# Two mixture stages of a fused network kernel: the first tile's projections move between the gate groups, the softmax and the choice of experts split into two parts, and the last sums change engine

## The reference

```python
x = x + attn_a0(layernorm(x))      # window attention
x = x + mixture(layernorm(x))      # the block of this case
x = x + attn_b0(layernorm(x))      # causal attention
x = x + mixture(layernorm(x))      # the block of this case, once more
x = x + attn_a1(layernorm(x))
x = x + stack(layernorm(x))        # six layers of local attention and feed-forward
x = x + attn_b1(layernorm(x))      # linear attention
x = x + stack(layernorm(x))

def mixture(x):                    # 8 experts, 2 of them for each row
    scores = softmax(x @ gate_w.T)
    weights, idx = top_k(scores, 2)
    xs = x[:, None, :] * weights[:, :, None]
    for e in range(8):
        h = silu(xs @ w1[e].T + b1[e])
        x2 = h @ w2[e].T + b2[e]
        x3 = xs @ w3[e].T + b3[e]
        y = y + sum(x2 * x3 * (idx == e))
    return y + silu(x @ sw1.T) * (x @ sw2.T) @ sw3.T
```

## Time and profile before

| | us |
|---|---|
| median of 3 runs | 4148.89 |
| the three runs | 4132.82, 4240.24, 4148.89 |
| the profiled execution's own time | 4147.29 |
| its span, first to last instruction | 4145.5 |
| busy: PE, VectorE, ScalarE, POOL | 3791.3, 2998.6, 2593.4, 2693.0 |

### The profile page before, as it was taken

The page is one execution under the profiler, slowest core; times in us unless marked ns, Lnnn a source line. Parts: engine busy times, 40 slices in busy tenths (PEclk is TensorE's granted clock), DMA queues, the critical chain, the costliest instruction groups (busy, mean ns, idle before and its releaser), DMA issues. The chain is left out here.

```text
span 4145.5 us, 159706 instructions
## 1 busy us (share of the span) xinstructions
PE 3791.3 (91%) x67305; PEld 2643.7 (64%) x67305; DVE 2998.6 (72%) x6173; ACT 2593.4 (63%) x4984; POOL 2693.0 (65%) x2315
## 2 busy tenths in 40 slices
PE   7897876999999999999999769999999999999997
PEld 5565543766666667676766436666666666676665
DVE  6675667777777777777777367777777777777773
ACT  4463443766667676666676336666766676766664
POOL 2193684776766767777777147767676767676773
PEclk9898887999999999999999769999999999999998
DMA  4000000333323333333233003333333233332222
GB/s 102 2 1 1 1 1 21 93 79 81 89 64 93 78 79 79 75 86 82 72 91 78 24 0 93 78 84 78 76 81 86 66 89 79 78 90 68 70 69 52
DMA packets 276305, 270.35 MB, mean 65 GB/s; under 512 B 131202, under 2 KB 174730, under 8 KB 275594
## 3 DMA queue, kind: packets, MB, share of 16 engines
q1 hardware_dynamic: 275594, 260.13, 25.2%
HBM read 51.57 MB, written 1.05 MB: 13 GB/s over the span
## 5 line engine op out<-in xcount | busy, mean ns | idle before, releaser
L1506 PE MATMUL PS<-l_wqkv,XNT 128*128 128x512 f32 x768 | 386.8, 626 | 0.8 <-issue 0.8
L1500 PE MATMUL PS<-l_wqkv,XNT 128*128 128x512 f32 x768 | 382.8, 621 | 0.5 <-issue 0.3
L1493 PE MATMUL PS<-l_wqkv,XNT 128*128 128x512 f32 x768 | 369.7, 604 | 4.1 <-ACT XNT L1703 2.5
L1668 ACT ACTIVATE l_sq<-PS 128x512 f32<-128x512 f32 x384 | 226.1, 596 | 196.0 <-PE PS L1500 156.0
L1668 ACT ACTIVATE m_sq<-PS 128x512 f32<-128x512 f32 x384 | 226.0, 596 | 194.0 <-PE PS L1500 156.4
L1947 POOL TENSOR_TENSOR m_Pm<-m_Pm,m_rs 128x1024 f32<-128x1024 f32 x96 | 182.7, 1903 | 228.7 <-DVE m_rs L1808 228.7
L1947 POOL TENSOR_TENSOR l_Pm<-l_Pm,l_rs 128x1024 f32<-128x1024 f32 x96 | 182.7, 1903 | 225.6 <-DVE l_rs L1808 225.6
L1795 DVE TENSOR_TENSOR l_QR<-PS,l_rot 128x512 f32<-128x512 f32 x192 | 131.8, 687 | 161.6 <-ACT l_sq L1668 161.6
L1795 DVE TENSOR_TENSOR m_QR<-PS,l_rot 128x512 f32<-128x512 f32 x192 | 131.8, 687 | 158.2 <-ACT m_sq L1668 158.2
L1826 DVE TENSOR_TENSOR XN<-PS,XN 128x128 f32<-128x128 f32 x192 | 56.1, 292 | 258.5 <-PE PS L1552 257.9
L1942 POOL TENSOR_TENSOR m_QR<-m_QR,m_UQ 128x1024 f32<-128x1024 f32 x96 | 227.7, 2372 | 20.1 <-DVE m_UQ L1798 20.1
(11 more groups left out here) (405 smaller groups left out, 11188.5 us busy)
## 6 DMA issues: line engine op xcount, KB each, us to landing
l_V<-l_Vt SPq DMA_DIRECT2D x576, 128.0 KB
m_V<-m_Vt SPq DMA_DIRECT2D x576, 128.0 KB
l_V<-l_Vt SPq DMA_DIRECT2D x384, 64.0 KB
m_V<-m_Vt SPq DMA_DIRECT2D x384, 64.0 KB
l_wqkv<-l_wqkv_dram SPq DMA_DIRECT2D x144, 128.0 KB, 2.4
l_rot<-l_rot_dram SPq DMA_DIRECT2D x48, 256.0 KB, 4.3
l_wo<-l_wo_dram SPq DMA_DIRECT2D x24, 256.0 KB, 3.6
l_w<-l_w_dram SPq DMA_DIRECT2D x12, 341.0 KB
```

Of the source, the lines that this page charges most:

```text
L1493: te.matmul(PS[:, b, :], tile_T(n), weights(n, b * 512, (b + 1) * 512), start=True, stop=True).then_inc(q_pr)
L1500: te.matmul(PS[:, 2 + b, :], tile_T(n), weights(n, INNER + b * 512, INNER + (b + 1) * 512), start=True, stop=True).then_inc(k_pr)
L1506: m = te.matmul(PS[:, r, :], tile_T(n), wv, start=True, stop=True)
L1668: ac.activation(sq[:, c, b * 512:(b + 1) * 512], PS[:, 2 * c + b, :], ACT.Square).then_inc(sq_out)
```

## The change

For the head of each mixture:

- TensorE: transposes of group 0, its gate products, transposes of group 1, `up(0)`, and then the rest of the groups, with the gate products of a group one step behind its transposes. All gate products go to bank 5; the transposes go to banks 6 and 7.
- VectorE: the gate values, the softmax and the choice are split into `FIRST` (tiles 0 to 3) and `OTHERS` (tiles 4 to 15). The softmax of the first part stands among the applications of the norm, its choice behind `up(0)`; the second part's softmax and comparison stand ahead of `gated(0)`, and the rest of its choice behind it.
- ScalarE: two exponentials in place of one. It no longer waits for the mask; POOL waits for it, ahead of its multiplication by the mask, at tiles 0 and 4.

For the end of each mixture: the three additions and the addition to `X` of tile 15 go from POOL to VectorE.

```diff
                 def pe():
-                    for g in range(NG):
-                        norm_turn(g, xn4[:, g % 2, :, :])
+                    def rows_turn(g):
+                        te.wait_ge(xn_out, g + 1)
+                        if g >= 2:
+                            te.wait_ge(xT_out, g - 1)
+                        for j in range(4):
+                            m = te.transpose(PS[:, 6 + g % 2, j * P:(j + 1) * P], xn4[:, g % 2, j, :], ident[:, :])
+                        m.then_inc(turn_mm)
+
+                    def gates(g):
                         te.wait_ge(xT_out, g + 1)
-                        for j in range(4):
-                            m = te.matmul(PS[:, 1 + g, j * E_N:(j + 1) * E_N], xt(4 * g + j), gate[:, :], start=True, stop=True)
+                        if g == 1:
+                            te.wait_ge(gate_out, 1)
+                        for i in range(4 * g, 4 * g + 4):
+                            m = te.matmul(PS[:, 5, i * E_N:(i + 1) * E_N], xt(i), gate[:, :], start=True, stop=True)
                         m.then_inc(gate_mm)
-                    te.wait_ge(gate_out, NG)
+
+                    rows_turn(0)
+                    gates(0)
+                    rows_turn(1)
+                    up(0)
+                    for g in range(2, NG):
+                        rows_turn(g)
+                        gates(g - 1)
+                    gates(NG - 1)
+                    te.wait_ge(gate_out, 2)
+                    te.wait_ge(xT_out, NG)
                     for i in range(NT + 1):
                         if i:
                             turn(i - 1)
                             shared_down(i - 1)
-                        if i < NT:
+                        if 0 < i < NT:
                             up(i)
...
                 def act():
-                    for g in range(NG):
-                        norm_copy(g, kept_T(g))
-                    ac.wait_ge(scores_out, 1)
-                    ac.activation(sc[:, :, :], sc[:, :, :], ACT.Exp).then_inc(sc_exp)
+                    def exponent(part, tiles):
+                        ac.wait_ge(scores_out, part + 1)
+                        ac.activation(sc[:, tiles, :], sc[:, tiles, :], ACT.Exp).then_inc(sc_exp)
+
+                    rows_copy(0)
+                    rows_copy(1)
+                    exponent(0, FIRST)
+                    rows_copy(2)
+                    rows_copy(3)
+                    exponent(1, OTHERS)
...
-                            if i == 0:
-                                ac.wait_ge(mask_out, 1)
...
                 def dve():
+                        if i == NT - 1:
+                            ve.wait_ge(y3_out, NT)
+                            for n in (4, 2, 1):
+                                V.step(ve.tensor_tensor(y[:, 0:n, :], y[:, 0:n, :], y[:, n:2 * n, :], ALU.add))
+                                V.wait()
+                            ve.wait_ge(zadd_out, NT)
+                            V.step(ve.tensor_tensor(X[:, i, :], X[:, i, :], y[:, 0, :], ALU.add))
...
+                    stats(0)
+                    stats(1)
+                    apply(0)
+                    stats(2)
+                    apply(1)
+                    stats(3)
+                    ve.wait_ge(gate_mm, 1)
+                    take_gates(FIRST)
+                    shifted_scores(0, FIRST)
+                    apply(2)
+                    scores(0, FIRST)
+                    apply(3)
+                    up(0)
+                    compare(FIRST)
+                    choose(FIRST)
+                    ve.wait_ge(gate_mm, NG)
+                    take_gates(OTHERS)
+                    shifted_scores(1, OTHERS)
+                    scores(1, OTHERS)
+                    compare(OTHERS)
+                    gated(0)
+                    choose(OTHERS)
...
                 def pool():
+                            if i in (0, 4):
+                                gp.wait_ge(mask_out, 1 + i // 4)
                             gp.tensor_tensor(x, x, over(mask[:, i, :], 2, [P, E_N, D]), ALU.mult).then_inc(x3m_out)
-                        if i:
+                        if 0 < i < NT:
```

More of the change, by code:

```diff
@@ L670, in dve, with take_gates, shifted_scores @@
                 def dve():
-                    all3, four = [P, NT, E_N], [P, NT, E_N, E_N]
-                    def scores():
-                        V.wait()
-                        V.step(ve.tensor_reduce(r1[:, :], sc[:, :, :], AX, ALU.max))
+                    def take_gates(tiles):
+                        ve.tensor_copy(sc[:, tiles, :], PS[:, 5, tiles.start * E_N:tiles.stop * E_N].rearrange("p (t e) -> p t e", e=E_N)).then_inc(gate_out)
+                    def shifted_scores(part, tiles):
+                        n = tiles.stop - tiles.start
+                        ve.wait_ge(gate_out, part + 1)
+                        V.step(ve.tensor_reduce(r1[:, tiles], sc[:, tiles, :], AX, ALU.max))
+                        V.wait()
+                        ve.tensor_tensor(sc[:, tiles, :], sc[:, tiles, :], over(r1[:, tiles], 2, [P, n, E_N]), ALU.subtract).then_inc(scores_out)
@@ L676, in scores @@
+                    def scores(part, tiles):
+                        n = tiles.stop - tiles.start
+                        ve.wait_ge(sc_exp, part + 1)
+                        V.step(ve.tensor_reduce(r1[:, tiles], sc[:, tiles, :], AX, ALU.add))
                         V.wait()
-                        ve.tensor_tensor(sc[:, :, :], sc[:, :, :], over(r1[:, :], 2, all3), ALU.subtract).then_inc(scores_out)
-                        ve.wait_ge(sc_exp, 1)
-                        V.step(ve.tensor_reduce(r1[:, :], sc[:, :, :], AX, ALU.add))
+                        V.step(ve.reciprocal(r1[:, tiles], r1[:, tiles]))
@@ L680, in scores, with compare @@
                         V.wait()
-                        V.step(ve.reciprocal(r1[:, :], r1[:, :]))
+                        V.step(ve.tensor_tensor(sc[:, tiles, :], sc[:, tiles, :], over(r1[:, tiles], 2, [P, n, E_N]), ALU.mult))
                         V.wait()
[L683 to L689, removed]
+                    def compare(tiles):
+                        n = tiles.stop - tiles.start
+                        four = [P, n, E_N, E_N]
+                        gt4, eq4 = (a[:, tiles, :].rearrange("p t (a b) -> p t a b", a=E_N) for a in (gt, eq))
+                        rival, own_s = over(sc[:, tiles, :], 2, four), over(sc[:, tiles, :], 3, four)
@@ L744, in dve @@
                             gated(i)
[L745 to L748, removed]
+                        down(i - 1)
                 def pool():
```

36 lines of the change are left out of this document (18 added, 18 removed).

## The result

The changed kernel's median is 4102.79 us (6 runs, 4095.65 to 4117.52), against 4145.02 us of before (6 runs, 4132.82 to 4240.24), so the medians are 42 us apart. The ratio of the means is 0.9909 with a 95% interval of 0.9885 to 0.9932, which is 38 us less, 0.9%. The forecast was 4127 us in a range of 4108 to 4152.

What follows compares the result with a forecast made beforehand. The prediction took POOL's late start and serial work to bound each mixture: 7.9 us from the head plus 2.6 from the end make 10.5, 21 us for two mixtures, giving 4127 us in a range of 4108 to 4152.

Steps and rivals of the forecast that it cites:

- What bounds a mixture: Each mixture: the wait until POOL can begin, POOL's work in series, then a barrier; other engines in the middle cost nothing.
- the term of the head: Start of each mixture: POOL begins tile 1 at 206.4 instead of 214.30 us, 7.9 us earlier.
- the 16 us downward: Range of the total time: some 16 us either side for a median of few runs, mostly downward.
- the rivals' 4139 and 4142: Total times if TensorE's clock stays low in the head (chance 0.15) or POOL's early start buys nothing (0.08).
- 10.0 plus 1.0 for transposes at the low clock: Head, POOL's start at tile 0 to tile 1: old 10.0 us plus 1.0 for tile 0's later, slow transposes.
- The end, 2.6 us: End of each mixture: VectorE doing tile 15's sums beside POOL gains between 2.2 and 2.9 us, taken as 2.6.
- The rule of two SBUF inputs: Mixture's end: GpSimd shares SBUF interfaces with VectorE for two-SBUF-input instructions; by it alone the gain would be 2.2 us.
- No effect elsewhere: Outside the edited parts: DMA share 0.01 or less, barriers keep their places, and the stacks do not see the change.
- The clock did not stay low: Rival in the head: TensorE at the low clock from 178.71 us, 4.3 us gained per mixture, 4139 us; chance 0.15.
- The early start was kept: Rival in the middle: TensorE or VectorE's second choice gives POOL new gaps, only the end counts, 4142 us; chance 0.08.
- the DMA queue of the stacks: Rival in the stacks: earlier starts slow the queue spreading `V`; 0.11 us per tile-layer takes back 21 us; chance 0.12.
- The table load: ScalarE's load before the silus in the head: 1.28 us, nothing added; the skill's page counts 1.38 us of drain beside it.

Runs made afterwards that it cites:

- the kernel with more work taken from POOL: Changed kernel with VectorE also adding every tile's sum to X and doing tile 15's bias and mask: 4129.99 us, ratio 0.9968.
- the end-only kernel: Kernel before with only its last sums moved from POOL to VectorE: 4135.65 us, ratio 0.9978.
- the one held back: Changed kernel with 13.1 us of idle POOL additions behind each mixture's last sums, so later stages start nearly as before: 4139.81 us, ratio 0.9988.
- the gate products one group behind: Kernel before with the mask wait moved from ScalarE to POOL and TensorE's gate products one group behind its transposes: 4119.44 us, ratio 0.9944.
- the mask's wait alone: Kernel before with one edit, POOL instead of ScalarE waiting for the mask at tile 0: 4130.88 us, ratio 0.9964.
- the kernel with the products behind the gates: Changed kernel with tile 0's products behind all gate products on TensorE, and behind the second softmax on VectorE: 4117.03 us, ratio 0.9938.

## Why the prediction was right in kind and too small

**What bounds a mixture.** Right. POOL's series is unchanged to 0.01 us over 121.5 us, and the mixtures' whole gain is POOL's start at tile 1 and the end behind VectorE's last product.

**The steps that failed.** Two. In the sum, the term of the head: 7.9 us in each mixture, where 10.6 and 11.4 were measured. In the range, the 16 us downward for the scatter of a median, where sets of the same changed kernel alone lie 19 us apart. From the forecast of 4127 to the median of 4102.8 us it is 24 us. About 4 are before's own median, which was 4148.9 in three runs and 4145.0 in six; 8 are the mixtures, 2 are causal attention, and the remaining 10 or so are the scatter of the other stages, which happened to be short in this set. Also, 4126 plus 1.6 is nearer to 4128 than to 4127, and the rivals' 4139 and 4142 leave out the 1.6; neither matters here.

**The head, 7.9 us forecast.** It was 10.6 us in the first mixture and 11.4 in the second. Here are its own steps in the first, counted from the mixture's start. The gates were to end at 18.9 us and ended at 17.6: `up(0)` began 0.2 us earlier, the clock rose earlier in it (5.71 us instead of 6.25), and the sets behind it overlapped (3.5 us instead of 4.0). From there to ScalarE's third product I had 4.2 us, and it was 3.8. POOL's tile 0 came at 23.6, not 25.3. The way from there to tile 1, 10.0 plus 1.0 for transposes at the low clock, was 9.9. The transposes are at the low clock indeed, but they start while ScalarE is still in the third product and end 0.9 us after it, and I had put the shared part's next product behind both. So the 1.0 was counted beside what covered it: from POOL's tile 0 to the start of tile 1's products it is 1.5 us instead of 1.25, and these products then take 5.04 us instead of 5.36. In the second mixture the transposes are at the low clock as well (1.92 us), and the way is still only 8.4 us, since tile 1's products take 3.60 there. What the forecast kept from before as a fixed 10.0 holds tile 1's products partly at the low clock.

**The end, 2.6 us.** It was 2.2. The lower value, from VectorE and POOL slowing one another for the whole stretch, was the right one: VectorE's three additions took 2.15 us beside POOL and 1.48 us in the kernel with more work taken from POOL, where POOL was idle then, and POOL's took 3.78. The rule of two SBUF inputs, cited in the prediction from the Trainium skill, went with that value.

**The sum.** 21 us forecast; 26.6 us between the first two profiles, and 28.6 against the three later profiles of before (349.5 against 320.8 us), whose second mixture is 2.5 us longer. I took one profile of before as if its mixtures were fixed to a tenth.

**No effect elsewhere.** Nearly right, and wrong in one place: causal attention behind the first mixture lasts 70.4 to 70.5 us in all five profiles of the changed kernel and 72.4 in all four of before. It is also 70.4 in the end-only kernel and 72.2 in the one held back. The mean clock, not the code, differs; first before, then changed:

```profile
344.06:416.51 72.45, 56.58 (x320) 41.50 (x320) 38.25 (x137) 28.37 (x65) 4.17 (x4) 0.90 0.00 1
```

```profile
329.50:399.94 70.44, 54.59 (x320) 40.06 (x320) 38.25 (x137) 28.32 (x65) 4.18 (x4) 0.93 0.00 1
```

The other kernels bear the clock out, but not that an earlier start is the shorter one: by the time at which the stage starts it lasts 70.4 us (from 329.5), 72.3 (336.1, the gate products one group behind), 70.1 (337.7, the mask's wait alone), 70.4 (340.3), 72.2 (342.0) and 72.4 (344.1), with a granted clock of 0.93 in the short ones and 0.90 in the long ones. What sets the level in a given execution I did not vary by itself, so that it is the start is argued, not shown.

**The range.** I took the 16 us downward from two close runs of before. Medians of the changed kernel over five sets go from 4101.6 to 4121.0 us, while those of before stayed between 4138 and 4145. 28.6 + 2.0 = 30.6 us is what the stages show as lasting, and the five distances between the medians of a set and before's beside it are 42, 24, 22, 37 and 34 us, 32 on average. Why the changed kernel has sets at two levels and the kernel before hardly does stays open: the sets at 4101.6 and 4104.3 us ran on one chip, those at 4120.4 and 4121.0 on two others, but other kernels had other stages of 3784 us on one of these as well.

**The rivals.** The clock did not stay low: 0.78 over `up(0)` and 1.00 over the gates behind it.

```profile
176.84:182.55 5.71, 5.71 (x13) 2.45 (x13) 5.45 (x22) 0.71 (x2) 0.49 (x1) 0.78 0.01 3
182.55:186.01 3.46, 3.46 (x33) 3.36 (x30) 1.37 (x4) 1.17 (x2) 0.00 (x0) 1.00 0.00 0
```

Nor does a low clock over the gates cost by itself what I had priced. The kernel with the products behind the gates had it over all gates, and lost 0 to 1.5 us per mixture, not 6, since it got the high clock afterwards; a case with all of it at the low clock, which the rival was, no run shows. The early start was kept, and the DMA queue of the stacks took nothing back: the stages that hold the two stacks last 3451.1 us together on average in five profiles of the changed kernel and 3450.9 in four of before. The table load cost its 1.28 us and no drain behind it, as the rows of before had said against the page of the Trainium skill that the prediction cites.

**What the parts are worth.** By the runs, first mixture, each part added to the ones before it: the mask's wait moved gives 5.2 us, the gates one group behind 1.7, the end 2.2, and the split of softmax and choice, with the choice ahead of POOL, the remaining 3.8 of the 12.9. No run has the split alone, so its price is the remainder, and in another order the parts would be priced differently: putting the mask's wait back into the finished head cost 3.6 us, not 5.2. Tile 0's products between the groups, the most visible part of the change, give 0 to 1.5.

## What to carry to other kernels

Where one engine is saturated behind a late start, price an edit by that engine's start at the first item behind which it never waits again, here tile 1 (a last wait at tile 2 was 0.5 us), and follow what covers what on the way there. Work that a slow shared neighbour makes expensive belongs ahead of that neighbour's first instruction; handing over more of it in the steady part can cost more than it takes away. And when a change is worth less than a per cent, compare stage by stage between barriers over several profiles: the edited stages repeated to 0.3 us in the changed kernel and to 2.5 us in the one before, while untouched ones moved the total by 20.

## What the hardware showed that I had not expected

The same code of linear attention lasted 91.8 to 105.1 us, with VectorE busy for 51.5 to 52.9 us and TensorE's busy time following its clock (72.2 us at 0.54, 63.8 at 0.59, 58.5 at 0.65). In the head, dense products moved 7.7 us later had the work behind them run at the high level (1.04 us instead of 1.92 for eight transposes), and that paid for the delay.

VectorE was slowed beside POOL in one instruction that has not two SBUF inputs but one. The last step of the second choice, a comparison with a constant on 96 elements with one input, took 1.26 us beside POOL's first addition; the same step took 0.18 us on 32 elements and, in the kernel before, 0.23 us on 128 elements while POOL was idle. It ended just after POOL's addition did (192.07 + 2.39 us), and took the same 1.26 us in the kernel with the products behind the gates. The reduction just ahead of it, with one input too, was not slowed: 0.95 us, all of it beside the same addition.

```profile
192.28 0.95 DVE L738 TENSOR_REDUCE f_mask<-f_gt 128x96 f32<-128x768 f32 x1
193.26 1.26 DVE L740 TENSOR_SCALAR f_mask<-f_mask 128x96 f32<-128x96 f32 x1
```
